# Powers of a recurrence: made in the output projection's stage and stored, or between the first sorted experts' tiles and kept on chip

## The reference

```python
A_t = jnp.power(A_c[None, :], t[:, None])         # t = 0 .. seq_len - 1
kernel = (C_c[None, :] * A_t * B_c[None, :]).T
y = ifft(fft(u) * fft(kernel))[..., :seq_len]      # a causal convolution
return y + D * u
```

## Time and profile before

| | |
|---|---|
| median of 3 runs | 3316.39 us (3313.81 to 3322.95) |
| the profiled execution | 3321.88 us, its span 3320.1 us |
| TensorE busy | 2796.0 us, 84% of the span |
| VectorE busy | 2213.3 us, 67% |
| ScalarE busy | 1846.6 us, 56% |
| GpSimd busy | 1484.9 us, 45% |
| mean granted clock of TensorE | 0.908 of full speed |

### The profile page before, as it was taken

One profiled execution on the slowest core, in us unless ns is written; L12 is line 12 of the kernel. 1 busy time (PEld: TensorE's weight loads), 2 busy tenths in 40 slices (PEclk: granted clock), 3 DMA queues, 4 the chain that ended last, 5 costly groups with the idle time before them and its releaser, 6 DMA issues. The chain is left out here.

```text
span 3320.1 us, 67732 instructions
## 1 busy us (share of the span) xinstructions
PE 2796.0 (84%) x21369; PEld 1304.9 (39%) x21370; DVE 2213.3 (67%) x3341; ACT 1846.6 (56%) x3190; POOL 1484.9 (45%) x1112
## 2 busy tenths in 40 slices
PE   5999999999999996899974499999996942476994
PEld 2333333333333333733333122222225942364772
DVE  5666666566666662988886799999982347535663
ACT  4555555555555552154455299999993654255432
POOL 1899999999999996400000011110112535441000
PEclk7999999999999997999996599999998975587995
DMA  2111111111111112600003312112214670262002
GB/s 81 32 50 43 57 44 44 50 43 53 49 44 50 43 47 88 225 1 1 0 2 112 75 41 51 44 44 50 45 40 146 189 211 28 67 180 58 11 13 57
DMA packets 275318, 208.27 MB, mean 63 GB/s; under 512 B 148846, under 2 KB 210726, under 8 KB 274320
## 3 DMA queue, kind: packets, MB, share of 16 engines
q1 hardware_dynamic: 266992, 192.77, 20.4%
q0 software_dynamic: 8224, 14.24, 1.3%
HBM read 125.43 MB, written 66.77 MB: 58 GB/s over the span
## 5 line engine op out<-in xcount | busy, mean ns | idle before, releaser
L604 DVE TENSOR_REDUCE attn_half_max<-attn_peek 128x2 f32<-128x1024 f32 x504 | 617.8, 1226 | 452.0 <-PE attn_peek L415 448.2
L353 POOL TENSOR_TENSOR attn_esum<-attn_esum,attn_prob 128x1024 f32<-128x1024 f32 x384 | 904.3, 2355 | 30.5 <-ACT attn_prob L521 4.6
L521 ACT ACTIVATE attn_prob<-attn_score 128x1024 f32<-128x1024 f32 x512 | 512.5, 1021 | 299.0 <-PE attn_score L389 297.0
L914 ACT ACTIVATE attn_prob<-attn_score 128x512 f32<-128x512 f32 x1024 | 556.3, 596 | 73.0 <-PE attn_score L864 58.9
L931 DVE TENSOR_REDUCE attn_half_max<-attn_peek 128x2 f32<-128x1024 f32 x512 | 583.7, 1217 | 11.0 <-PE attn_peek L850 11.0
L447 PE MATMUL attn_acc<-attn_prob,attn_v 128*64 128x512 f32 x2048 | 489.0, 599 | 0.1
L880 PE MATMUL attn_acc<-attn_prob,attn_v 128*32 128x256 f32 x4096 | 328.3, 392 | 12.1 <-ACT attn_out L906 10.6
L1803 POOL DMA_INDIRECT sorted_x<-attn_sent_rows,attn_send x64 | 62.5, 976 | 555.8 <-PE attn_score L864 555.8
L850 PE MATMUL attn_peek<-attn_ke,attn_qe 48*128 48x512 bf16 x1024 | 203.0, 393 | 45.0 <-DMA attn_ke<-k 30.0
L447 PEld LDWEIGHTS attn_acc<-attn_prob,attn_v 128*64 128x64 f32 x2048 | 131.2, 137 | 208.0 <-issue 163.5
L864 PE MATMUL attn_score<-attn_qe,attn_ke 49*128 49x512 bf16 x1024 | 200.8, 389 | 8.4 <-ACT attn_prob L914 5.5
(11 more groups left out here) (552 smaller groups left out, 4299.5 us busy)
## 6 DMA issues: line engine op xcount, KB each, us to landing
experts_w<-in_L_ffn_W SPq DMA_DIRECT2D x80, 256.0 KB
attn_xb<-attn_x_all SPq DMA_DIRECT2D x64, 256.0 KB, 2.6
attn_invB<-inv SPq DMA_DIRECT2D x64, 256.0 KB
o<-attn_out SPq DMA_DIRECT2D x32, 512.0 KB, 2.7
out_o<-o SPq DMA_DIRECT2D x8, 2048.0 KB
experts_w<-in_L_ffn_w SPq DMA_DIRECT2D x40, 256.0 KB
mix_f<-picked SPq DMA_DIRECT2D x16, 512.0 KB, 7.3
experts_x<-sorted_x SPq DMA_DIRECT2D x112, 65.0 KB
```

The lines of the kernel that those rows point to most:

```text
L353: nc.gpsimd.tensor_tensor(own, before, prob[:, u % NPROB, :, :], ALU.add).then_inc(added, 1)
L521: nc.scalar.activation(prob[:, u % NPROB, :, :], score[:, u % 2, :, :], ACT.Exp).then_inc(exped, 1)
L604: V.tensor_reduce(half_max[:, :, t, half], first_look(m) if first else peek[:], AX.X, ALU.max, negate=True).then_inc(maxed, 1)
L914: nc.scalar.activation(prob[:, n % NPROB, :], score[:, n % RING, :], ACT.Exp).then_inc(exped, 1)
```

## The change

`SsmPowers` is split. `SsmTurns` keeps the six loads, the columns, the root and GpSimd's squarings, in the projection's stage as before; its tiles now live until the program's end. `SsmPowers` keeps the fill of `decay`, the doublings and the weighing, and moves as a whole to VectorE's stream of the first sorted experts' stage. Its buffer (five times 1024 columns) is opened ahead of that stage and stays until the second sorted experts' stage has ended, so the stores, the scratch tensor, the loads and the waits for them go. What is computed is the same.

The pieces go behind the following tiles; VectorE's straight code is two rounds longer for it (tiles 12 to 19), the other engines' isn't:

| behind the body of tile | that is, after `experts_y` of | piece |
|---|---|---|
| 12 | 11 | `begin`: decay and the first column |
| 13, 14, 15 | 12, 13, 14 | doublings 0 and 1, 2 and 3, 4 and 5 |
| 16, 17, 18, 19 | 15, 16, 17, 18 | doubling 6, 7, 8, 9 |
| 68, 69 | 67, 68 | `weigh`, real part; imaginary part |

```diff
             gated.load(sp, gated_in)
-            job.store(sp)
             sp.wait_ge(gated_in, gated.LOADS * DMA)
...
             job.begin(dve, nc)
-            for k in range(3):
-                job.double(dve, k)
             dve.wait_ge(consts, 2 * DMA)
...
             take(5)
-            for k in range(3, 6):
-                job.double(dve, k)
             take(6)
             for n in range(NT // 8):
                 dve.wait_ge(b_turned, n + 1)
                 V.tensor_copy(cT[:, n * 8 * P:(n + 1) * 8 * P]...).then_inc(b_copied, 1)
-                if n < 2:
-                    job.double(dve, 6 + n)
-            for k in range(8, job.LOG):
-                job.double(dve, k)
-            job.weigh()
             take(7)
...
-        def iterations(eng, body, between=None):
+        def iterations(eng, body, between=None, start=3):
             for u in range(UNROLL):
                 body(u, u, True, False)
-            START = 3 if between else 1
+            START = start if between else 1
             for n in range(1, START):
+                if between and n == 3:
+                    between()
                 for u in range(UNROLL):
                     body(UNROLL * n + u, u, False, False)
-            if between:
+            if between and START == 3:
                 between()
...
+            def grow(n):
+                if n == 12:
+                    powers.begin(dve)
+                elif 13 <= n <= 15:
+                    for k in range(2 * (n - 13), 2 * (n - 12)):
+                        powers.double(k)
+                elif 16 <= n <= 19:
+                    powers.double(n - 10)
+                elif n == blocks - UNROLL or n == blocks - UNROLL + 1:
+                    powers.weigh(n - blocks + UNROLL)
...
             if job:
-                iterations(dve, with_division, attention)
+                iterations(dve, with_division, attention, 5)
...
-            for n in (0, 1, 4, 2, 3):
-                sp.dma_start(kept[:, n, :], powers_d[:, n, :]).then_inc(kept_in[n], DMA)
             sp.dma_start(dd[:], column(skip)).then_inc(skip_in, DMA)
```

More of the change, by code:

```diff
@@ L1877, in take, with sorted_experts_stage @@
                                      self.bias_b[:].unsqueeze(1).to_broadcast([P, len(own), D]), ALU.add).then_inc(self.summed, 1)
-def sorted_experts_stage(nc, name, ident, blocks, xs_d, expert_d, weights, y_d, beside=None):
+def sorted_experts_stage(nc, name, ident, blocks, xs_d, expert_d, weights, y_d, beside=None, grown=None):
     E = 8
@@ L2414, in _, with __init__, within @@
                 step(m)
-class SsmPowers:
+class SsmTurns:
     LOG = SEQ.bit_length() - 1
[L2422 to L2432, removed]
+    def __init__(self, ctx, nc, A_r, A_i, B_r, B_i, C_r, C_i):
+        self.vecs = (A_r, A_i, B_r, B_i, C_r, C_i)
+        sb = lambda name, shape: ctx.enter_context(nc.sbuf_tensor(f"turns_{name}", shape, F32))
+        self.par, self.cols = sb("par", [P, 6]), sb("cols", [P, 13])
+        self.turns, self.turn_tmp = sb("turns", [P, 3, self.LOG]), sb("tmp", [P, 3])
+    def within(self, st):
+        self.par_in, self.step, self.squared, self.rooted = (st.sem(n) for n in ("par_in", "step", "squared", "rooted"))
+        self.based, self.turn_step = st.sem("based"), st.sem("turn_step")
+        return self
     def load(self, sp):
@@ L2436, in load @@
             sp.dma_start(self.par[:, n:n + 1], column(vec)).then_inc(self.par_in, DMA)
[L2438 to L2443, removed]
     def root(self, act, nc):
@@ L2536, in square, with __init__, within, begin @@
                 link(G.tensor_tensor(sn, sn, t, ALU.mult))
-            G.tensor_scalar(self.turn(2, k), sn, -1.0, 0.0, ALU.mult, ALU.add).then_inc(self.turned, 1)
-    def double(self, dve, k):
+            link(G.tensor_scalar(self.turn(2, k), sn, -1.0, 0.0, ALU.mult, ALU.add))
+class SsmPowers:
+    KEPT = 5
+    def __init__(self, ctx, nc, turns):
+        self.nc, self.turns = nc, turns
+        self.kept = ctx.enter_context(nc.sbuf_tensor("powers", [P, self.KEPT, SEQ], F32))
+    def within(self, st):
+        self.tmp, self.tmp2, self.grown = st.sb("tmp", [P, SEQ]), st.sb("tmp2", [P, SEQ]), st.sem("grown")
+        return self
+    def begin(self, dve):
+        self.V, self.link = self.nc.vector, Chain(dve, self.grown)
+        V, link, decay = self.V, self.link, self.kept[:, 4, :]
+        link(V.memset(decay, 1.0))
+        link(V.tensor_scalar(decay, decay, self.turns.r, None, ALU.mult))
+        link(V.memset(self.kept[:, 0, 0:1], 1.0))
+        link(V.memset(self.kept[:, 1, 0:1], 0.0))
+    def double(self, k):
         V, link, n = self.V, self.link, 1 << k
         Er, Ei, tmp, tmp2 = self.kept[:, 0, :], self.kept[:, 1, :], self.tmp, self.tmp2
-        c, sn, nsn = (self.turn(part, k) for part in range(3))
-        dve.wait_ge(self.turned, k + 1)
+        c, sn, nsn = (self.turns.turn(part, k) for part in range(3))
         link(V.tensor_scalar(tmp[:, 0:n], Er[:, 0:n], c, None, ALU.mult))
@@ L3557, in recurrent_block_kernel @@
                                     a["L0_ffn_gate_w"], a["L0_ffn_gate_bias"],
-                                    lambda st: SsmPowers(st, *inputs("L2_attn_", "A_real A_imag B_real B_imag C_real C_imag"), powers, gated.powers, gated.stored), gated)
+                                    turns.within, gated)
             fT = held.enter_context(nc.sbuf_tensor("fT", [P, TOK], F32))
```

72 lines of the change are left out of this document (24 added, 48 removed).

## The result

| | before | after |
|---|---|---|
| median, 20 runs of each side by side | 3318.62 us (3313.81 to 3327.03) | 3327.99 us (3323.66 to 3332.74) |
| the profiled execution | 3321.88 us, span 3320.1 | 3332.74 us, span 3331.0 |
| projection's stage | 94.6 us | 89.1 us |
| dispatch and projection stage | 79.4 us | 85.8 us |
| first sorted experts' stage | 192.5 us | 207.4 us |

The ratio is **1.0027 (1.0021 to 1.0033)**: 9 us slower. A stage's length is the distance of its first instruction from that of the next stage; a sorted experts' stage is counted from SyncE's issue of the load of `experts_raw_b`, 0.7 us behind its first issue. The prediction was +4.8 us, 3321.2, with a range to 3329.

What follows compares the result with a forecast made beforehand. VectorE was taken to bound the projection's tail and TensorE the first sorted experts' loop. Terms -6.1 + 0 + 8.2 + 2.7 gave +4.8 us on 3316.4, so 3321.2 us, range 3311 to 3329.

Steps and rivals of the forecast that it cites:

- B: Rival, first sorted experts' stage: TensorE's clock falls in its gaps, transfers late, growth a tenth longer; +10.8 us, 3327.2; chance 0.12.
- projection's stage: Tail of that stage: earlier copies let product 7 start 3.9 us earlier, until weight loads bind; gain 6.1 us.
- combining stage: Five loads leave SyncE's queue there; taken at nothing, up to 0.5 us of gain for the range.
- middle, VectorE's results late: First sorted experts' stage, tiles 11 to 21: growth delays VectorE's results and TensorE's second product of tile 21; +8.2 us.
- middle, late transfers: Same experts' stage: late results hold up GpSimd's keeping and SyncE's row and weight loads; up to 1 us more.
- tail: End of the experts' stage, from tile 67's result: weighing delays the last results and GpSimd's last send; +2.7 us.
- the head saves nothing: Projection's stage: removing decay and doublings 0 to 2 gains nothing, since later takes and transposes wait for product 6.
- A: Rival, experts' stage: register load stays hidden beneath the last growth step; sum -2.1 us, 3314.3; chance 0.15.
- C: Rival, projection's stage: product 7 starts no earlier, only take(7) gains, 1.3 us; sum +9.6, 3326.0; chance 0.07.
- D: Rival, outside these stages: tiles opened later move in SBUF and device memory; a few us either way; chance 0.08.
- The two rules: Trainium skill, on VectorE: semaphores after Vector operations cost nothing extra; GpSimd contends for shared SBUF interfaces, lengthening sends within the late-transfer bound.

## Why the prediction was right or wrong

The time lies within the range, but 1 us from its upper end and above the forecast's own band of 3317 to 3325.5. The sum had +4.8 us and the medians give +9.4 (the ratio +9.0), so it was 4.2 to 4.6 us short. Another 2.2 us lie in the base: the forecast stood on a median of three runs, 3316.4, and the median of the twenty of the same kernel is 3318.6. The range held because it was made wide enough for rivals that didn't come. The prediction contradicts itself there too: it takes B, at 3327.2, into the range to 3329 and then lays most of B above it. By its steps, against the stages of the profile after:

| step | predicted | measured |
|---|---|---|
| projection's stage | -6.1 | -5.5 (94.6 to 89.1); mean of all profiles -5.4 |
| combining stage | 0 | +0.2 (172.2 to 172.4) |
| middle, VectorE's results late | +8.2 | +9.3 |
| middle, late transfers | 0, bound +1 | +1.7 |
| tail | +2.7 | +3.3 |
| sum | +4.8 | +9.0 (medians: +9.4) |

**The projection's stage** went as told: the gap 1.21 us (1.3), product 7 at 1375.76, 3.2 behind the end of product 6 at 1372.58, 7.36 long, the loads late next. The mechanism was right and the term 0.6 too big: the last weights landed at 1386.3 where 1386.5 was reckoned, but the stage had begun 0.8 us earlier in this profile (1298.5 against 1299.3). That the head saves nothing is shown by the kernel with the head kept.

**The middle's mechanism** was right, the 128.4 to 128.6 us of every kernel without growth between the tiles show it. Its size was short in two terms. The growth itself took 15.1 us (15.3), so the durations read in the old place held in the new one. The rest was reckoned at 11.1 us (8 x 1.35 + 0.3) and took 12.3 of the 27.4 between the results of tiles 11 and 19: 0.5 ahead of the first piece, seven results at 0.27, seven loads and bias steps at 0.78 + 0.39, and 1.65 behind the last doubling at the loop's entry, where the load took 1.13 and the bias step's end was waited for 0.22. Tile 21's second product was hence 9.3 late and not 8.2. The estimate of 0.7 for the load came from a row where something else still ran beneath it.

**The late transfers** were the step that failed: they were put at nothing in the sum and at 1 in the bounds. The run with the sends moved shows 1.7. The prediction had named the chain (send, keep, row load) but had not followed it to its end: the weights of the tile before stand behind the row load in SyncE's queue, so the late result of tile 19 shows up once more in the weights of tile 26, five tiles behind the last product that a result held up. The size is that of one pair of profiles: in the kernel with the weighing last the same stretch lost another 0.8 us.

**The tail** cost 3.3 and not 2.7: again 0.78 to 0.80 for the load, and the lengthened sends (1.98 us), which were not in it. The last one, not beside a weighing, ends 2.4 us behind tile 71's result, 2.2 before, so they cost only 0.2 here; in the kernel with the weighing last it ends 3.2 behind, 1.1 later than before.

**The rivals.** A, the hidden load, is refuted by the bracket of 0.78 behind every piece, and by the load moved ahead. B had the time nearly right (3327.2 against 3328.0), and C the change (+9.6 against +9.4), both by luck and by the wrong road. For B the granted clock stayed at 1.00 in this window and in the 20 us ahead of it, which hold all the late results,

```profile
2592.60:2612.60 20.00, 15.04 (x123) 14.16 (x124) 9.10 (x25) 8.96 (x36) 10.21 (x16) 1.00 0.53 148
```

and of its three parts only the late transfers came. C is refuted by product 7. D shows no trace: without growth the steady part is the old one to 0.1 us. What stays open is 1 us or so: the five series with nothing of the growth on the path lie 3 to 5.6 us below the kernel before (0.9991 to 0.9983) where the stages give 5.4. The intervals take that in; so would a dispatch stage at its longer lengths a little more often.

**The two rules.** Behind each piece the row shows 0.78 us without work. The Trainium skill ("VectorE: DVE Perf Modes", The DRAIN you can't avoid) says a semaphore after each Vector operation costs nothing extra; the trace agrees between Vector steps and not for the register load behind them. Sends took 0.97 us as a rule. The six that began 0.14 to 0.39 us behind the start of a weighing step with two tensors as inputs, 1.28 us long, took 1.80 to 1.99 (after, sends three tiles later, weighing last, one step a tile); two that began 0.26 us ahead of such a step took 1.07 and 1.08 (the register load ahead); and three that began 0.12 behind a step with one tensor, 0.75 long, took 1.47 to 1.48 (the growth in the waits for loads). In the six and the three the delay is about what was left of the instruction, less 0.1. Two sends in whose midst a step with one tensor began (0.42 and 0.43 behind their start) took 1.28 and 1.29 and that step no longer than elsewhere, which this doesn't explain. The Trainium skill ("SBUF — State Buffer", SBUF: two separate sides) says that VectorE and GpSimd lock a shared pair of ports for a whole instruction, so that the one that comes second waits, and describes a transfer issued by GpSimd as held up by VectorE's 2-port modes. The order and the size of the delays agree with the lock; that the steps with two inputs hold up a send as well is what these runs add.

## What to carry to other kernels

Work for an engine that isn't the bound belongs in the places where that engine itself stands idle, and its own timeline lists them: here growth and weighing cost 14 us between tiles that left 0.5 us each, and nothing in the waits for loads at the start of the same stage. When a result comes late, follow every queue behind it to its last entry, not to the first that it delays: the weights behind the row load behind the destinations behind the send. And read a stage of varying load time (61.7 to 64.7 us here) apart from the steady one, or the noise of one hides an edit in the other.

## What the runs showed of the hardware

- A register load behind a wait of VectorE's own stream costs 0.78 us until the next instruction starts; ahead of the chain it still costs 0.31 to 0.4, in the gap or the later start of the first step; at the loop's entry it was 1.13.
- A scatter issued by GpSimd takes 0.97 us; begun behind the start of a VectorE instruction of 128x1024 it took 1.80 to 1.99 where that had two tensors as inputs (six sends) and 1.47 to 1.48 where it had one (three sends); begun 0.26 us ahead of one with two inputs it took 1.07 and 1.08 (two sends).
- TensorE's granted clock fell from 2.4 to 1.2 GHz in the midst of unbroken work, at different moments of the same stage in different executions, and with 45, 55 or 58 us at 1.2 GHz that stage was 79.4, 82.1 to 82.6 or 85.7 us long: steps of 3.2 us, a third of what the change did to the whole kernel.
